# The experts' first positions in the sorted list: summed along the columns on VectorE, in place of two products on TensorE

## The reference

```python
out = jnp.einsum('btc,oc->bto', x, W_base) + b_base
h = jnp.einsum('btc,erc->bter', x, As)
x = x + out + jnp.einsum('bter,eor,be->bto', h, Bs, w) * 2.0
# second layer, on the new x
rw = softmax(router_logits)                 # 16 x 8
w, sel = top_k(rw, 2); w = w / w.sum(-1)
dense_w = zeros(16, 8).at[b, sel].add(w)
for e in range(8):                          # gate, up 128x512, down 512x128
    acc += dense_w[:, e] * ((gelu(x @ gate[e]) * (x @ up[e])) @ down[e])
x = x + acc + (gelu(x @ sh_gate) * (x @ sh_up)) @ sh_down
```

## Time and profile before

| | |
|---|---|
| median of 3 runs | 130.63 us (130.32 to 130.80) |
| the profiled execution's own time | 131.27 us |
| its span, first to last instruction | 129.6 us |
| busy: PE, PEld | 124.8 us (96%), 113.9 us (88%) |
| busy: DVE, ACT, POOL | 90.7 us (70%), 72.1 us (56%), 62.4 us (48%) |
| granted TensorE clock, mean | 1.000 |
| HBM | 107 GB/s over the span |

### The profile page before, as it was taken

One profiled execution on the slowest core, in us unless ns is written; L12 is line 12 of the kernel. 1 busy time (PEld: TensorE's weight loads), 2 busy tenths in 40 slices (PEclk: granted clock), 3 DMA queues, 4 the chain that ended last, 5 costly groups with the idle time before them and its releaser, 6 DMA issues.

```text
span 129.6 us, 3162 instructions
## 1 busy us (share of the span) xinstructions
PE 124.8 (96%) x873; PEld 113.9 (88%) x873; DVE 90.7 (70%) x177; ACT 72.1 (56%) x136; POOL 62.4 (48%) x111
## 2 busy tenths in 40 slices
PE   6999999999999989999999999999999999999991
PEld 5956977878878858999999999999999999999990
DVE  2696798769979999633377758767777677766641
ACT  2259767976876768113466485657565756611110
POOL 5455964645797947453344632653365513610000
PEclk9999999999999999999999999999999999999999
DMA  3997788599400086579745586558799950013921
GB/s 53 286 337 272 191 289 295 189 260 291 117 3 0 14 249 225 166 273 415 291 190 228 230 326 248 207 200 324 253 311 313 390 190 0 3 33 135 285 66 53
DMA packets 14524, 26.56 MB, mean 205 GB/s; under 512 B 2224, under 2 KB 7600, under 8 KB 12976
## 3 DMA queue, kind: packets, MB, share of 16 engines
q1 hardware_dynamic: 14192, 26.35, 60.5%
q10 hardware_dynamic: 320, 0.07, 0.2%
HBM read 12.52 MB, written 1.31 MB: 107 GB/s over the span
## 4 chain that ended last, share of the span: by engine, by line
PE 93%; DVE 2%; issue 1%; ACT 1%; DVEq 0%; ACTq 0%
PE bank L1049 11%; PE bank L1085 9%; PE bank L1086 9%; PE bank L1087 9%; PE bank L1067 6%; PE bank L996 5%; PE bank L998 5%; PE bank L997 5%; PE bank L1107 5%; PE bank L1108 4%; PE bank L1109 4%; PE bank L1012 3%; PE bank L920 3%; PE bank L928 3%; PE bank L895 3%; PE bank L1013 2%
## 5 line engine op out<-in xcount | busy, mean ns | idle before, releaser
L556 ACT ACTIVATE work<-bank 128x512 f32<-128x512 f32 x48 | 28.7, 599 | 39.8 <-PE bank L1087 17.2
L714 DVE TENSOR_TENSOR bank<-bank,work 128x512 f32<-128x512 f32 x40 | 27.9, 698 | 18.5 <-PE bank L1087 13.0
L731 DVE TENSOR_TENSOR hT_lo<-bank,hT_hi 128x512 fp32r<-128x512 f32 x40 | 27.3, 681 | 1.0 <-issue 0.5
L483 POOL TENSOR_TENSOR wstd<-wexd,wstd 128x512 fp32r<-128x512 f32 x12 | 15.6, 1298 | 24.3 <-ACT wstd L598 24.3
L1085 PE MATMUL bank<-xp,wst 128*128 128x256 f32 x96 | 27.2, 284 | 0.0
L1086 PE MATMUL bank<-xp,wst 128*128 128x256 f32 x96 | 27.2, 283 | 0.0
L1087 PE MATMUL bank<-xp,wst 128*128 128x256 f32 x96 | 27.2, 283 | 0.0
L565 ACT CAST hT_hi<-bank 128x512 fp32r<-128x512 f32 x40 | 23.3, 582 | 1.6 <-DVE bank L714 1.6
L1086 PEld LDWEIGHTS bank<-xp,wst 128*128 128x128 f32 x96 | 18.4, 192 | 0.0
L1085 PEld LDWEIGHTS bank<-xp,wst 128*128 128x128 f32 x96 | 18.4, 192 | 0.0
L1087 PEld LDWEIGHTS bank<-xp,wst 128*128 128x128 f32 x96 | 18.4, 192 | 0.0
(11 more groups left out here) (153 smaller groups left out, 214.9 us busy)
## 6 DMA issues: line engine op xcount, KB each, us to landing
wst<-wex SPq DMA_DIRECT2D x12, 1024.0 KB, 4.8
raw_ex<-n_L_cond_skill_gate_dram SPq DMA_DIRECT2D x8, 256.0 KB, 3.2
raw_ex<-in_L_cond_skill_up_dram SPq DMA_DIRECT2D x8, 256.0 KB, 4.2
sst<-n_L_cond_skill_gate_dram SPq DMA_DIRECT2D x8, 256.0 KB, 3.4
sst<-in_L_cond_skill_up_dram SPq DMA_DIRECT2D x8, 256.0 KB, 4.3
xn<-in_x_dram SPq DMA_DIRECT2D x4, 256.0 KB, 4.5
out_dram<-xT SPq DMA_DIRECT2D x4, 256.0 KB, 2.7
sst<-_L_cond_shared_gate_dram SPq DMA_DIRECT2D x1, 256.0 KB, 4.9
```

What stands on the lines that cost most here:

```text
L556: act.activation(gelu_sb[q], gate_ps[q][:, :], ACT.Gelu_apprx_tanh).then_inc(gelu_done, 1)
L714: dve.tensor_tensor(up_ps[u][:, :], up_ps[u][:, :], gelu_sb[q], ALU.mult).then_inc(h_done, 1)
L731: dve.tensor_tensor(hT_lo[:, q, :], up_ps[u][:, :], f32(hT_hi[:, q, :]), ALU.subtract).then_inc(lo_done, 1)
```

## The change

The two products of `sort_starts`, ACT's copy of their result and POOL's two instructions for `par` go. The counts `n` are now made with the operands of the product exchanged, so that every partition holds the counts of all experts along its columns. DVE's comparisons then need only 8 experts (16 x 64) and one more small instruction gives `par`. Behind `gated(1)` DVE multiplies both (twice the pairs, and the odd ones) with a constant table `below` (16 x 144), sums along the columns to `starts` (16 x 18) and marks in `pos_e[:, 0]` whether a row is its expert's left-over. POOL has one position instruction fewer. `sort_singles` takes over the wait for `x1lo_ready`. POOL's constants change: the 16 x 24 table `upick` is replaced by `below`, filled by two memsets and made by two selects in place of three. The later counts of the semaphores are renumbered. The comparisons and the products of DVE use the memory of `rows`, which is written later.

```diff
             pool.memset(ones[:, :], 1.0).then_inc(const_fill, 1)
-            pool.memset(upick[:, :, :], 2.0).then_inc(const_fill, 1)
+            pool.memset(below[:, 0, :, :], 2.0).then_inc(const_fill, 1)
+            pool.memset(below[:, 1, :, :], 1.0).then_inc(const_fill, 1)
...
-            pool.affine_select(out=upick[:, 0, :], in_=upick[:, 0, :], compare_op=ALU.is_gt, fill=0.0,
-                               base=0, pattern=[[1, 8]], channel_multiplier=-1).then_inc(consts, 1)
...
+            for i in range(2):
+                pool.affine_select(out=below[:, i, :, :], in_=below[:, i, :, :], compare_op=ALU.is_gt, fill=0.0,
+                                   base=0, pattern=[[1, 9], [-1, 8]], channel_multiplier=0).then_inc(consts, 1)
...
-            pool.wait_ge(sort_sum, 2)
-            pool.tensor_scalar(par[:, :], half[:, :], -2.0, None, ALU.mult).then_inc(sort_step, 1)
-            pool.wait_ge(sort_step, 4)
-            pool.tensor_tensor(par[:, :], par[:, :], rank_n[:, 1, :], ALU.add).then_inc(sort_step, 1)
-            pool.wait_ge(sort_sb, 2)
-            pool.tensor_tensor(pos_e[:, 0, :], rank_n[:, 0, 0:8], starts[:, 2, :], ALU.subtract).then_inc(sort_step, 1)
...
+            pool.wait_ge(sort_sum, 5)
+            pool.tensor_tensor(pos_e[:, 1, :], rank_n[:, 0, 0:8], starts[:, 0, 0:8], ALU.add).then_inc(sort_step, 1)
+            pool.tensor_scalar(pos_e[:, 2, :], starts[:, 1, 0:8], starts[:, 0, 8:9], None, ALU.add).then_inc(sort_step, 1)
+            pool.wait_ge(sort_step, 5)
+            pool.tensor_tensor(pos_e[:, 2, :], pos_e[:, 2, :], pos_e[:, 1, :], ALU.subtract).then_inc(sort_step, 1)
+            pool.wait_ge(sort_step, 6)
+            pool.wait_ge(sort_sum, 6)
+            pool.tensor_tensor(pos_e[:, 2, :], pos_e[:, 0, :], pos_e[:, 2, :], ALU.mult).then_inc(sort_step, 1)
+            pool.wait_ge(sort_step, 7)
+            pool.tensor_tensor(pos_e[:, 3, :], pos_e[:, 1, :], pos_e[:, 2, :], ALU.add).then_inc(sort_step, 1)
...
                     gelu(t, c % 2)
-                    if g == 0 and c == 2:
-                        act.wait_ge(sort_mm, 2)
-                        act.copy(starts[:, :, :], start_ps[0:B, 0:24].rearrange("p (a b) -> p a b", a=3)
-                                 ).then_inc(sort_sb, 1)
...
                     if g == 0 and c == 0:
-                        dve.wait_ge(consts, 8)
+                        dve.wait_ge(consts, 7)
                         dve.wait_ge(sort_sb, 1)
-                        dve.tensor_tensor(n_ge[:, :, :],
-                                          rank_n[:, 1, :].rearrange("p (b a) -> p b a", a=1).to_broadcast([B, B, 8]),
+                        n = rank_n[:, 1, 0:8]
+                        dve.tensor_tensor(n_ge, n.rearrange("p (e a) -> p e a", a=1).to_broadcast([B, 8, 8]),
+                                          thr[:, :].rearrange("p (a r) -> p a r", a=1).to_broadcast([B, 8, 8]),
+                                          ALU.is_ge).then_inc(sort_sum, 1)
                         dve.wait_ge(sort_sum, 1)
-                        dve.tensor_reduce(half[:, :], n_ge[:, :, :], AXIS_X, ALU.add).then_inc(sort_sum, 1)
+                        dve.tensor_reduce(twos_odd[:, 0, :], n_ge, AXIS_X, ALU.add).then_inc(sort_sum, 1)
+                        dve.wait_ge(sort_sum, 2)
+                        dve.scalar_tensor_tensor(twos_odd[:, 1, :], twos_odd[:, 0, :], -2.0, n, ALU.mult, ALU.add
+                                                 ).then_inc(sort_sum, 1)
+                    if g == 0 and c == 1:
+                        dve.wait_ge(sort_sum, 3)
+                        dve.tensor_tensor(in_front, twos_odd[:, :, :].rearrange("p i (a e) -> p i a e", a=1)
+                                          .to_broadcast([B, 2, 9, 8]), below[:, :, :, :], ALU.mult).then_inc(sort_sum, 1)
+                        dve.wait_ge(sort_sum, 4)
+                        dve.tensor_reduce(starts[:, :, :], in_front, AXIS_X, ALU.add).then_inc(sort_sum, 1)
+                        dve.scalar_tensor_tensor(pos_e[:, 0, :], twos_odd[:, 0, :], 2.0, rank_n[:, 0, 0:8],
+                                                 ALU.mult, ALU.is_equal).then_inc(sort_sum, 1)
...
-                pe.matmul(count_ps[0:B, B:2 * B], memb_sum[:, :], ones[:, 0:B], start=True, stop=True).then_inc(sort_mm, 1)
-            def sort_starts():
-                pe.wait_ge(sort_sum, 2)
-                pe.wait_ge(sort_step, S_PAR)
-                pe.wait_ge(x1lo_ready, NG)
-                pe.matmul(start_ps[0:B, 0:24], half[:, :], upick[:, :, :].rearrange("p a e -> p (a e)"),
-                          start=True, stop=False)
-                pe.matmul(start_ps[0:B, 8:16], par[:, :], ltri[:, 0:8], start=False, stop=True).then_inc(sort_mm, 1)
+                pe.matmul(count_ps[0:B, B:2 * B], ones[:, 0:B], memb_sum[:, :], start=True, stop=True).then_inc(sort_mm, 1)
             def sort_singles():
                 pe.wait_ge(sort_step, S_CLASS)
+                pe.wait_ge(x1lo_ready, NG)
...
                     gate_up_shared(g, c)
-                    if g == 0 and c == 2:
-                        sort_starts()
```

More of the change, by code:

```diff
@@ L78, in lora_then_top2_moe @@
         ltri = sb("ltri", [B, B])
-        upick = sb("upick", [B, 3, 8])
+        below = sb("below", [B, 2, 9, 8])
         memb = sb("memb", [B, 2, B])
@@ L82, in lora_then_top2_moe @@
         rank_n = sb("rank_n", [B, 2, B])
[L83 to L86, removed]
+        twos_odd = sb("twos_odd", [B, 2, 8])
+        starts = sb("starts", [B, 2, 9])
         pos_e = sb("pos_e", [B, 4, 8])
@@ L94, in lora_then_top2_moe @@
         rows = sb("rows", [B, 2, 3, 32])
+        spare = rows[:, :, :, :].rearrange("b k v n -> b (k v n)")
+        n_ge = spare[:, 0:64].rearrange("b (e r) -> b e r", e=8)
+        in_front = spare[:, 0:144].rearrange("b (i f e) -> b i f e", i=2, f=9)
         wlist = sb("wlist", [P, 32])
@@ L340, in _ @@
                       allow_small_or_imprecise_dtypes=True).then_inc(consts, 1)
-            pool.wait_ge(const_fill, 4)
+            pool.wait_ge(const_fill, 5)
             pool.affine_select(out=ltri[:, :], in_=ltri[:, :], compare_op=ALU.is_gt, fill=0.0,
                                base=0, pattern=[[1, B]], channel_multiplier=-1).then_inc(consts, 1)
-            pool.affine_select(out=upick[:, 0, :], in_=upick[:, 0, :], compare_op=ALU.is_gt, fill=0.0,
-                               base=0, pattern=[[1, 8]], channel_multiplier=-1).then_inc(consts, 1)
[L347 to L350, removed]
+            for i in range(2):
+                pool.affine_select(out=below[:, i, :, :], in_=below[:, i, :, :], compare_op=ALU.is_gt, fill=0.0,
+                                   base=0, pattern=[[1, 9], [-1, 8]], channel_multiplier=0).then_inc(consts, 1)
             pool.iota(thr[:, :], pattern=[[2, 8]], base=2, channel_multiplier=0,
@@ L354, in _ @@
                       allow_small_or_imprecise_dtypes=True).then_inc(consts, 1)
-            pool.wait_ge(consts, 8)
+            pool.wait_ge(consts, 7)
             pool.wait_ge(rt_step, 4)
@@ L415, in _ @@
                                ALU.mult).then_inc(sort_step, 1)
-            pool.wait_ge(sort_sum, 3)
+            pool.wait_ge(sort_sum, 7)
             pool.tensor_scalar(single[:, :], pos[:, :], float(LEFT), None, ALU.is_ge).then_inc(sort_step, 1)
-            pool.wait_ge(sort_step, 12)
+            pool.wait_ge(sort_step, 10)
             pool.tensor_tensor(twice[:, 0:1], single[:, 0:1], single[:, 1:2], ALU.mult).then_inc(sort_step, 1)
             pool.tensor_tensor(twice[:, 2:3], single[:, 0:1], single[:, 1:2], ALU.add).then_inc(sort_step, 1)
-            pool.wait_ge(sort_step, 14)
+            pool.wait_ge(sort_step, 12)
             pool.tensor_scalar(twice[:, 3:4], twice[:, 0:1], -2.0, None, ALU.mult).then_inc(sort_step, 1)
-            pool.wait_ge(sort_step, 15)
+            pool.wait_ge(sort_step, 13)
             pool.tensor_tensor(twice[:, 1:2], twice[:, 2:3], twice[:, 3:4], ALU.add).then_inc(sort_step, 1)
@@ L440, in _ @@
             pool.tensor_scalar(lp[:, 5:6], lp[:, 0:1], float(LEFT), None, ALU.add).then_inc(sort_step, 1)
+            pool.wait_ge(sort_step, 19)
+            pool.tensor_copy(lp[:, 3:4], lp[:, 4:5]).then_inc(sort_step, 1)
+            pool.wait_ge(sort_step, 20)
+            pool.tensor_scalar(lp[:, 6:8], lp[:, 2:4], twice[:, 0:1], lp[:, 5:6], ALU.mult, ALU.add).then_inc(sort_step, 1)
             pool.wait_ge(sort_step, 21)
-            pool.tensor_copy(lp[:, 3:4], lp[:, 4:5]).then_inc(sort_step, 1)
+            pool.tensor_tensor(lp[:, 8:10], lp[:, 6:8], pos[:, :], ALU.subtract).then_inc(sort_step, 1)
             pool.wait_ge(sort_step, 22)
-            pool.tensor_scalar(lp[:, 6:8], lp[:, 2:4], twice[:, 0:1], lp[:, 5:6], ALU.mult, ALU.add).then_inc(sort_step, 1)
+            pool.tensor_tensor(lp[:, 10:12], lp[:, 8:10], single[:, :], ALU.mult).then_inc(sort_step, 1)
             pool.wait_ge(sort_step, 23)
```

(10 more changed lines are left out.)

16 lines of the change are left out of this document (4 added, 12 removed).

## The result

The changed kernel took 130.71 us (median of 20 runs, 130.56 to 131.23), the kernel before 130.43 us beside it (20 runs, 130.26 to 130.84). The ratio is 1.0022, with an interval of 1.0014 to 1.0031: 0.28 us slower, small but clear of noise. The forecast was 0.22 us faster, so the sign is wrong.

What follows compares the result with a forecast made beforehand. PE was taken to bound the kernel (93% of the chain). Its 0.38 us saving, less DVE's delay beyond 0.41 us (0.52) and 0.05 for restarting, gave 0.22: 130.63 - 0.22 = 130.41 us, range 130.05 to 130.95.

Steps and rivals of the forecast that it cites:

- What leaves PE: Around sort_starts, 19.25 to 20.09 us on PE: removing the two small products saves 0.84 - 0.46 = 0.38 us.
- what comes onto DVE: Behind gated(0) the added work is hidden; behind gated(1) product, sum and mark take 0.285, 0.29 and 0.155 us.
- a rival feared that POOL might hold it up: DVE's left-over mark around 20.10 us waits for POOL's 0.20 us instruction: no gain or small loss, 130.61 to 130.87; chance 0.14.
- d: Delay of gated(2) on DVE by the new work, from 19.70 to 20.22 us: 0.52 us, bounds 0.38 and 0.78.
- The net gain at 22 us: At PE's down product of step 1: 0.74 us less the delay of gated(2), giving 0.22 us.
- One sign: Near 21.5 us PE waits 0.1 to 0.2 us for DVE's low part; down product of step 1 starts near 21.65.
- its 0.05 for a restart: After PE's wait before the down product of step 1, the next matmul comes later, at a cost of 0.05 us.
- ACT, POOL's position chain and the setup: ACT loses a 0.17 us copy, POOL's chain starts at 20.26, setup has 1.13 us of idle cover: no cost.
- Does the gain reach the end: After 22 us PE mostly waits only for itself, so the 0.22 us offset is carried to the end.
- the changed order of port claims: A new DVE and POOL collision later in the kernel costs up to about 0.9 us, 131.3; chance 0.05.
- The basis of the sum: Profiled execution of 131.27 us, 0.64 above the median; the 0.22 us gain was taken off the median, 130.63.
- The rival by which a changed order gains 0.55 us: At 43.18 us DVE's packing goes before POOL, ending PE's 0.55 us wait at 46.30: 129.86 us; chance 0.06.

Runs made afterwards that it cites:

- changed, packing free: Changed kernel with POOL's x1_whole(3) and up_lo(4) moved behind its wait for the list, so POOL is idle when DVE packs: 130.15 us; run again, 130.23 us.
- the kernel with the packing free: Kernel before with POOL's x1_whole(3) and up_lo(4) moved behind its wait for the list: 130.46 us, ratio 0.9996.

## Why the prediction was wrong

These are the starts of matmuls on PE, read from the timelines of the profiled executions (us; the first shared matmul, the third, eleventh and thirteenth down product, the first single, the first slot). The long arrangement is the kernel before once more, the short one the run with the DVE memset at 38 us, the changed kernel its second profile:

| kernel | time | shared | 3rd | 11th | 13th | single | slot |
|---|---|---|---|---|---|---|---|
| before, long arrangement | 131.16 | 15.22 | 23.88 | 41.43 | 46.22 | 49.06 | 61.51 |
| before with the memset, short arrangement | 130.33 | 15.22 | 23.90 | 41.45 | 45.53 | 48.25 | 60.67 |
| changed | 130.71 | 15.23 | 23.59 | 41.18 | 45.73 | 48.53 | 61.01 |
| before, four more on DVE | 130.98 | 15.22 | 23.90 | 41.45 | 46.01 | 48.85 | 61.29 |
| changed, packing free | 130.12 | 15.21 | 23.58 | 41.23 | 45.31 | 48.03 | 60.45 |

**What leaves PE, and what comes onto DVE: right.** The removal was put at 0.38 us, and two products put back cost 0.31 to 0.34 where DVE's block is in place. The small instructions came out within 0.02 us of their estimates, and the mark, of which a rival feared that POOL might hold it up, took 0.14 us. The term that was off is d: 0.43 us in place of 0.52, because the sum and the mark started 0.03 to 0.04 us earlier than worked out and `gated(2)` 0.07 us behind the mark in place of 0.12. The net gain at 22 us was to be 0.22 and is 0.31. One sign failed here: PE was to wait 0.1 to 0.2 us for the low part of step 1 and did not, since that part ended at 21.34 and PE's matmul started at 21.45; PE lost the 0.09 us in the step that followed, for which the forecast had only its 0.05 for a restart. ACT, POOL's position chain and the setup were hidden as worked out; the larger constants left POOL 0.84 us of idle time in place of 1.13.

**Does the gain reach the end: wrong.** The text said that both engines "are released by the same chain and should shift together", and gave the changed order of port claims a chance of 0.05 on the slow side. The table shows what happened. Against the short arrangement the changed kernel is 0.31 us ahead at the third down product and 0.27 at the eleventh, and 0.20 behind at the thirteenth and 0.34 at the first slot: 130.68 against 130.34 is that 0.34. Against the long arrangement it is ahead from the third down product on, and 0.5 ahead from the thirteenth, which is what the profiles alone showed. So the step that failed is that the engines shift together. The instructions that the change adds to DVE moved a stand of 0.4 us from `gated(6)` to `gated(5)`; this put POOL 0.4 us ahead of DVE; and in all four profiles of the changed kernel without the move (two of them with a small addition) DVE's packing finds POOL's instruction 0.34 to 0.40 us under way (42.45 and 42.83) and takes 0.92 to 0.99 us. In the kernel before it depended on some hundredths of a us at 38 us whether it took 0.17 or 1.18. The price of the collision is 130.98 - 130.35 = 0.63 us, from the run with four memsets, and 0.31 of it is paid back.

**The basis of the sum: wrong.** The prediction noted that the profiled execution was 0.64 us over the median and used the difference only to shift the result. That difference was the clue: the row of 1.18 us at 43.18, on which a rival was built, belonged to an arrangement whose time, 131.2 us, none of the 20 timed executions of that session had. The rival by which a changed order gains 0.55 us described what the kernel before already did in 10 of these 20 executions (130.26 to 130.35), and there it was worth 0.85.

The rule of the Trainium skill (SBUF — State Buffer, Who interferes with whom) that was held against the change near 20 us did apply, but at 43 us: the packing reads two SBUF inputs, POOL's `x1_whole` reads SBUF, and by the rule they exclude each other for a whole instruction, by the order of issue. The trace agrees with it: the packings of 1.18 and 0.95 us end at 44.36 and 43.78, each 0.03 us after POOL's instruction (44.33 and 43.75), and the one of 0.17 us starts ahead of POOL's. The starts in a profile do not always tell whose turn it is: at 37.96 and 37.97 POOL is listed first and waits.

**Open.** Why DVE stands for 0.4 us was not found: that added instructions ahead of it move it is shown, the cause is not. The Trainium skill (Advanced Engine Details and Errata, ISA Cache) says that an engine's instructions are cached in lines of 256; a change of line might fit, but no row here shows one at that place. The trace of the kernel before has no packet of an instruction queue between 25 and 31 us. Open too is the spacing of 0.2 us between executions at 130.35 and 130.56, which the kernel with the packing free has as well. The tie at 45.3 us is a candidate: of the four profiles with the packing free it costs DVE 0.48 us in one and nothing in three (0.14 us each), and no run removes it. Nor is it known why the tie at 38 us fell, by the times, the long way in 29 of 30 executions of one measurement and in one of 96 of the others.

## What to carry to other kernels

Before summing against a profiled execution, look at where its own time lies in the spread of the runs; if the runs form groups, the profile shows one group, and its stalls may be absent from the others. Where two engines claim the same port within a few hundredths of a microsecond, a change anywhere ahead can decide the order, and that can be worth more than the change: list such near ties, and remove them by order in the queue before measuring small edits. A gain of 0.3 us that a trace shows at its place can be real even where the total says otherwise; with the collision out of the way 0.2 to 0.3 us of it reached the end.

## What the runs showed of the hardware that was not expected

- Four one-element memsets on an idle DVE at 1 us made the kernel 0.4 us slower (130.98 against 130.57), by moving a stand of about 0.4 us from `gated(6)` to `gated(5)`.
- A scalar_tensor_tensor of 16 elements takes 0.17 us free and 0.95 to 1.20 us when a POOL instruction of 1.3 us has started 0.13 to 0.38 us ahead of it.
- The DVE instruction behind the small mark starts 0.07 us after it (20.00 and 20.07), though the mark lasts 0.14.
- The stage ahead of 15 us is 0.3 us longer in some executions (first shared matmul at 15.54 and 15.57 in two profiles, else 15.12 to 15.28).
